# Threshold search with bf16 totals: counts read as their upper 16 bits, each over 256 columns

## The chip, the cores and the metric

The kernel runs on one core of one Trainium2 chip. The metric is the time of one execution on the device, in microseconds (us). A core has five engines with queues of their own: TensorE (PE, with its weight loads listed as PEld), VectorE (DVE), ScalarE (ACT), GpSimd (POOL) and SyncE (SP), which issues transfers. They meet only through semaphores.

## The reference, cut to what matters

A chain of six blocks with residuals on 4 x 1024 tokens of 256 features: an int4 feed-forward, a multi-scale attention, the feed-forward again, a mixture of experts (MoE), a linear attention, and the MoE again with the same weights. The change is in the MoE, which runs twice:

```python
T = 4096; E = 32; cap = int(1.25 * T / E)                # 160
probs = softmax(gelu(ri @ r1_w.T + r1_b) @ r2_w.T)
topp, topi = top_k(probs, 2)
routed = hit.any(1)                                       # the token picked this expert
score = where(routed, probs, -inf)
idx = argsort(-score, axis=0)[:cap].T                     # each expert takes its best 160 tokens
...
xe = xf[idx]; up = xe @ w_up.T; gate, upv = split(up)
ye = (silu(gate) * upv) @ w_down.T
out = zeros.at[idx].add(w * ye)
```

So for each of 32 experts the 160 best of 4096 scores must be found.

## The kernel before, in words

The kernel doesn't sort. Per expert it looks for the score's threshold: the value over which at most 160 scores lie. It does so for 16 experts at a time (a "half", class `Choice`): 128 partitions are 8 parts x 16 experts, and each partition holds 512 scores (`COLS`) of its expert, turned into numbers whose high 16 bits are searched first and then the low ones. One round tries three thresholds at once and gains a factor of four; there are `ROUNDS` = 15 rounds, 7 on the high and 8 on the low bits.

A round k:
- `counts` (VectorE) counts, per partition, how many scores are below the middle threshold, tries[2], over 512 columns (L1442, sum to `under[:, 0:1]`), and with `split` also those below tries[1] over the first 256 columns (L1440, sum to `part`). Then it prepares `ahead` (L1446), the part of the next thresholds that doesn't depend on the outcome.
- `signs` (ScalarE) sums signs of (tries[1] - score), over the second 256 columns with `split` and over 512 without (L1577), and of (tries[3] - score) over 512 columns (L1579), into `under[:, 1:2]` and `under[:, 2:3]`. Counting over a sum of signs is the same up to a factor and a constant.
- `total` (TensorE) adds the 8 parts of each expert and hands every partition the total: a product with `same_e`, a 128x128 matrix of ones and zeros in fp32 as weights, and the sums as 3 moving columns (L1603). With `split` two products come before it into the same PSUM columns: the constant `may_under` (L1598), which moves the limit to zero, and `part` with `twice_e`, which is 2 x same_e (L1600). An fp32 product runs as two passes, each with its own weight load: two records each.
- `decide` (VectorE) compares with the limit (L1452 with `split`; L1454 and L1455 without) and writes the next thresholds (L1456), for which ScalarE, VectorE and TensorE wait.

The first half's search (`split`) runs in `route`, before any expert: nothing else is on TensorE. On VectorE each round has a companion after its counts (`beside(k)`): rounds 3 and 4 make the second half's scores (L2122, L2126), rounds 5 to 8 their sums (L1409), rounds 9 to 13 the tokens' shares. GpSimd works on `values` (L1558, L1560), started once the picks are known. After the search the order is ties, scan, ranks, positions, tables, lists, all on VectorE and TensorE in turns, and then GpSimd gathers the rows of the first experts (L1346).

The second half's search (without `split`) runs in `experts`, laid by `with_steps` into the fixed order of the first 16 experts' work: TensorE runs `up` products (L2369) and `down` products (L2382) of the experts, and a total stands between two `up` pairs. VectorE's product of gate and value (L2493) waits for ScalarE's gate (L2422). All queues are strictly in this order.

The constants (`same_e`, `before_e`, `twice_e`) are made once by GpSimd in `RouterSetup.constants`, at the beginning of the attention.

Of the kernel before, what the change touches and what calls it, by code (L numbers as in the profile page):

```python
# [17 lines left out]
ALU = mybir.AluOpType  # L18
ACT = mybir.ActivationFunctionType
F32 = mybir.dt.float32  # L20
# [5 lines left out]
P = 128  # L26
# [1194 lines left out]
class RouterSetup:  # L1221
# [18 lines left out]
    def constants(self, nc, pool):  # L1240
        s, ints, pool_chain = self.s, self.ints, self.pool_chain
        chain = Chain(pool, pool_chain)
        at = 0
        for out, pattern, base, step in ((s.e_down, [[-1, EXPERTS]], EXPERTS, 0),
                                         (s.tile_no, [[1, 2 * TILES]], 0, 0), (s.row_no, [[0, 1]], 1, 1)):
            n = pattern[0][1]
            chain.link(nc.gpsimd.iota(ints[:, at:at + n], pattern, base=base, channel_multiplier=step))
            chain.link(nc.gpsimd.tensor_copy(out[:], ints[:, at:at + n]))
            at += n
        chain.link(nc.gpsimd.iota(ints[:, at:at + ST_TILES], [[P, ST_TILES]], base=TOKENS + 1, channel_multiplier=1))  # L1250
        chain.link(nc.gpsimd.tensor_copy(s.spare_no[:], ints[:, at:at + ST_TILES]))
        chain.link(nc.gpsimd.tensor_copy(self.mine[:, 0:HALF], s.ident[:, 0:HALF]))
        for j in range(1, PARTS):
            chain.link(nc.gpsimd.tensor_tensor(self.mine[:, 0:HALF], self.mine[:, 0:HALF], s.ident[:, HALF * j:HALF * (j + 1)], ALU.add))
        chain.link(nc.gpsimd.tensor_copy(s.same_e[:].rearrange("p (j e) -> p j e", e=HALF), self.mine[:, 0:HALF].rearrange(
            "p (o e) -> p o e", o=1).broadcast_to([P, PARTS, HALF])))
        chain.link(nc.gpsimd.tensor_copy(s.fold[:], s.ident[:, 0:VALUES * HALF]))
        for j in range(1, P // (VALUES * HALF)):
            chain.link(nc.gpsimd.tensor_tensor(s.fold[:], s.fold[:], s.ident[:, VALUES * HALF * j:VALUES * HALF * (j + 1)], ALU.add))
        chain.link(nc.gpsimd.iota(ints[:, 0:P], [[1, P]], base=1, channel_multiplier=0))  # L1260
        chain.link(nc.gpsimd.tensor_copy(self.mine[:], ints[:, 0:P]))
        chain.link(nc.gpsimd.tensor_scalar(s.before_e[:], self.mine[:], s.row_no[:, 0:1], None, ALU.is_gt))
        chain.link(nc.gpsimd.tensor_tensor(s.before_e[:], s.before_e[:], s.same_e[:], ALU.mult))
        chain.link(nc.gpsimd.tensor_scalar(s.twice_e[:], s.same_e[:], 2.0, None, ALU.mult))
        chain.link(nc.gpsimd.memset(s.half[:], 0.5))
        chain.link(nc.gpsimd.memset(s.tiny[:], 1e-6))
        chain.link(nc.gpsimd.iota(ints[:, at:at + 4], [[1, 4]], base=0, channel_multiplier=0))
        chain.link(nc.gpsimd.tensor_copy(s.tries_no[:], ints[:, at:at + 4]))
        chain.link(nc.gpsimd.memset(s.may_under[:, 0:1], float(CAP - TOKENS) / PARTS))
        chain.link(nc.gpsimd.memset(s.may_under[:, 1:2], float(2 * CAP - TOKENS - TOKENS // 2) / PARTS))  # L1270
        chain.link(nc.gpsimd.memset(s.may_under[:, 2:3], float(2 * CAP - TOKENS) / PARTS))
        chain.link(nc.gpsimd.memset(s.limit[:, 0:1], float(TOKENS - CAP)))
        chain.link(nc.gpsimd.memset(s.limit[:, 1:3], float(TOKENS - 2 * CAP)))
# [9 lines left out]
def alloc_moe(nc, s):  # L1283
    sb = nc.alloc_sbuf_tensor
    s.r1 = sb("r1", [P, CC, HIDDEN], F32)
    s.r1s = sb("r1s", [STATS, HIDDEN], F32)
    s.r1b = sb("r1b", [HIDDEN, 1], F32)
    s.r2 = sb("r2", [HIDDEN, EXPERTS], F32)
    s.e_down = sb("e_down", [P, EXPERTS], F32)
    s.tile_no = sb("tile_no", [P, 2 * TILES], F32)  # L1290
    s.row_no = sb("row_no", [P, 1], F32)
    s.spare_no = sb("spare_no", [P, ST_TILES], F32)
    s.same_e = sb("same_e", [P, P], F32)
    s.before_e = sb("before_e", [P, P], F32)
    s.twice_e = sb("twice_e", [P, P], F32)
    s.half = sb("half", [P, TILES], F32)
    s.tiny = sb("tiny", [P, 1], F32)
    s.tries_no = sb("tries_no", [P, 4], F32)
    s.may_under = sb("may_under", [P, 3], F32)
    s.limit = sb("limit", [P, 3], F32)  # L1300
    s.fold = sb("fold", [P, VALUES * HALF], F32)
    s.xn_rows = nc.dram_tensor("xn_rows", (TOKENS, ROW), F32, kind="Internal").ap()
    s.x_sum = nc.dram_tensor("x_sum", (TOKENS + SPARE, C), F32, kind="Internal").ap()
# [58 lines left out]
class Choice:  # L1362

    def __init__(self, nc, s, m, half, earlier=None):
        self.nc, self.s, self.m, self.half = nc, s, m, half
        st, name = m.st, f"c{half}_"

        def sb(n, shape, dt=F32):  # L1370
            return st.sb(name + n, shape, dt)
        self.score, self.above = sb("score", [P, COLS]), sb("above", [P, COLS])
        if earlier is None:
            self.equal, self.n_above, self.n_equal = (sb(n, [P, COLS]) for n in ("equal", "n_above", "n_equal"))
            self.junk = sb("junk", [P, 2, COLS], BF16)
        else:
            self.equal, self.n_above, self.n_equal, self.junk = earlier.equal, earlier.n_above, earlier.n_equal, earlier.junk
        self.tries, self.ahead = sb("tries", [P, 4]), sb("ahead", [P, 4])
        self.under, self.part, self.passed = sb("under", [P, 3]), sb("part", [P, 1]), sb("passed", [P, 3])
        self.steps, self.level, self.quota, self.one = (sb(n, [P, 1]) for n in ("steps", "level", "quota", "one"))  # L1380
        self.count, self.base = sb("count", [P, 2]), sb("base", [P, 2])
        self.pos = sb("pos", [P, 2, TILES], BF16)
        self.by_place = sb("by_place", [P, CAP])
        self.quads = QUADS_E // 2
        self.tiles = SLOT_TILES // 2
        self.held = sb("held", [P, VALUES, self.tiles])
        self.token = sb("token", [P, self.tiles])
        self.added, self.spare = (sb(n, [P, self.quads, 2, ST_TILES]) for n in ("added", "spare"))
        self.of_any, self.whole = sb("of_any", [P, self.quads, ST_TILES]), sb("whole", [P, self.quads, ST_TILES], I32)
        (self.scored, self.score_turned, self.score_copied, self.halved, self.high_made, self.low_made, self.tried, self.parted,  # L1390
         self.counted, self.signed, self.totaled, self.tied, self.offset, self.placed, self.place_turned, self.pos_made,
         self.valued, self.hot_made, self.slotted, self.copied, self.listed, self.rows_known, self.slots_made, self.dve) = (
            st.sem(name + n) for n in (
                "scored", "score_turned", "score_copied", "halved", "high_made", "low_made", "tried", "parted", "counted", "signed",
                "totaled", "tied", "offset", "placed", "place_turned", "pos_made", "valued", "hot_made", "slotted", "copied", "listed",
                "rows_known", "slots_made", "dve"))
        self.bank, self.score_bank = 4, 6 + half
# [36 lines left out]
    def counts(self, v, k, split):  # L1434
# [4 lines left out]
        if split:  # L1439
            nc.vector.tensor_scalar(self.n_above[:, 0:COLS // 2], self.score[:, 0:COLS // 2], self.tries[:, 1:2], None, ALU.is_lt,  # L1440
                                    ALU.add, accum_out=self.part[:]).then_inc(self.parted, 1)
        nc.vector.tensor_scalar(self.above[:], self.score[:], self.tries[:, 2:3], None, ALU.is_lt, ALU.add,  # L1442
                                accum_out=self.under[:, 0:1]).then_inc(self.counted, 1)
        units = HIGH + LOW
        unit = 0.5 if k + 1 in (len(HIGH), ROUNDS) else float(units[k + 1])
        nc.vector.tensor_scalar(self.ahead[:], self.s.tries_no[:], unit, self.tries[:, 0:1], ALU.mult, ALU.add)  # L1446
# [147 lines left out]
    def total(self, pe, k, split):  # L1594
        nc, s, totals = self.nc, self.s, self.s.ps[:, self.bank, 0:3]
        pe.wait_ge(self.tried, self.turn_of(k))
        if split:
            nc.tensor.matmul(totals, s.same_e[:], s.may_under[:], start=True, stop=False, skip_group_check=True)  # L1598
            pe.wait_ge(self.parted, k + 1)
            nc.tensor.matmul(totals[:, 1:2], s.twice_e[:], self.part[:], start=False, stop=False, skip_group_check=True)  # L1600
        pe.wait_ge(self.counted, k + 1)
        pe.wait_ge(self.signed, k + 1)
        nc.tensor.matmul(totals, s.same_e[:], self.under[:], start=not split, stop=True,  # L1603
                         skip_group_check=True).then_inc(self.totaled, 1)

    def offsets(self, pe):
        nc, s = self.nc, self.s
# [1417 lines left out]
```

## Time and profile before

| | before |
|---|---|
| median of 3 runs | 1800.84 us (1800.36 to 1804.57) |
| profiled execution | 1800.5 us, of which span 1798.8 us |
| TensorE busy | 1506.6 us (84%) |
| VectorE busy | 968.8 us (54%) |
| ScalarE busy | 729.0 us (41%) |
| GpSimd busy | 563.1 us (31%) |
| mean granted TensorE clock | 0.907 |

The profile is of one execution; its records name engine, line, operation and tiles. "Idle before" is the idle time of the engine in front of a record, with what ended it. A group whose records repeat is merged, with its count. The ends of TensorE's records are modelled. Granted clock 1.00 is 2.4 GHz, 0.50 is 1.2 GHz.

### The profile page before, as it was taken

The numbers are of one execution on the slowest core, as the hardware profiler recorded it, in microseconds if no ns is written. First come the engines' busy times: TensorE is split into PE (matmuls) and PEld (weight loads), VectorE is DVE, ScalarE is ACT, GpSimd is POOL, SyncE is SP. The second block draws the span as 40 slices with busy tenths as digits, with TensorE's granted clock in tenths as the row PEclk, the third lists the DMA queues.
The fourth block names the chain that finished last, engine by engine and source line by source line (L and its number), as shares of the span: only waits on it lengthen the run. The fifth ranks groups of instructions, "written<-read, shape, count | busy, mean of one in ns | idle before, by whom it ended". The sixth has DMA issues, their size and how long they took to land. (4 is left out here: it accounts for less than half of the span.)

```text
span 1798.8 us, 26975 instructions
## 1 busy us (share of the span) xinstructions
PE 1506.6 (84%) x9512; PEld 1150.9 (64%) x9512; DVE 968.8 (54%) x2696; ACT 729.0 (41%) x1775; POOL 563.1 (31%) x466
## 2 busy tenths in 40 slices
PE   6899989999998677549999996589995559999994
PEld 5566544555554554439989996355553549899994
DVE  8766677787883597755531111356565754521110
ACT  4222147666666385415323232123433425322331
POOL 6522200000000441221646445222111231637545
PEclk9998989999999898559999998799996569999997
DMA  3042462333300031325879974410113225879974
GB/s 103 18 144 111 119 125 55 78 55 79 55 26 2 19 111 62 146 46 187 229 205 248 257 230 64 129 36 24 47 47 124 76 71 191 231 215 248 265 193 46
DMA packets 113492, 212.10 MB, mean 118 GB/s; under 512 B 20085, under 2 KB 79386, under 8 KB 104154
## 3 DMA queue, kind: packets, MB, share of 16 engines
q1 hardware_dynamic: 87066, 178.93, 31.4%
q0 software_dynamic: 26304, 31.60, 11.5%
q8 instruction: 69, 1.13, 0.3%
q14 instruction: 53, 0.43, 0.1%
HBM read 158.71 MB, written 51.38 MB: 117 GB/s over the span
## 5 line engine op out<-in xcount | busy, mean ns | idle before, releaser
L952 DVE TENSOR_REDUCE attnm_top<-psum 128x1 f32<-128x384 f32 (+3 forms) x384 | 212.9, 597 | 56.7 <-PE psum L1037 52.6
L1174 ACT ACTIVATE attnm_prob<-psum 128x512 f32<-128x512 f32 (+1 forms) x384 | 192.1, 530 | 88.8 <-PE psum L1047 82.2
L2493 DVE SCALAR_TENSOR_TENSOR moe2e_h<-moe2e_gate,psum 128x160 f32<-128x160 f32 x160 | 50.6, 321 | 203.0 <-ACT moe2e_gate L2422 173.4
L2314 POOL DMA_INDIRECT out<-moe2e_y,moe_scatter_i x76 | 118.7, 1562 | 130.9 <-ACT moe2e_y L2448 69.9
L2493 DVE SCALAR_TENSOR_TENSOR moe1e_h<-moe1e_gate,psum 128x160 f32<-128x160 f32 x160 | 50.6, 321 | 202.6 <-ACT moe1e_gate L2422 161.0
L2314 POOL DMA_INDIRECT x_sum<-moe1e_y,moe_scatter_i x76 | 119.1, 1567 | 129.3 <-ACT moe1e_y L2448 71.5
L2369 PE MATMUL psum<-moe2e_xgT,moe_w_up 128*128 128x160 f32 x1024 | 152.4, 304 | 2.4 <-ACT moe2e_xgT L2438 2.4
L2369 PE MATMUL psum<-moe1e_xgT,moe_w_up 128*128 128x160 f32 x1024 | 152.2, 304 | 2.4 <-ACT moe1e_xgT L2438 2.4
L2369 PEld LDWEIGHTS psum<-moe2e_xgT,moe_w_up 128*128 128x128 f32 x1024 | 144.0, 193 | 4.8 <-issue 4.8
L2369 PEld LDWEIGHTS psum<-moe1e_xgT,moe_w_up 128*128 128x128 f32 x1024 | 143.9, 193 | 4.8 <-issue 4.8
L1346 POOL DMA_INDIRECT moe_xg<-xn_rows,moe_gather_i x80 | 84.3, 1054 | 168.3 <-DVE moe_gather_i L1531 102.0
L938 POOL TENSOR_TENSOR attnm_tail_v<-attnm_v_tail,attnm_tail_p 128x256 f32<-128x256 f32 x32 | 19.8, 620 | 343.9 <-PE psum L1089 284.4
L1035 PE MATMUL psum<-attn_mask_ts,ident_bf 128*128 128x128 bf16 x512 | 105.4, 226 | 10.2 <-DVE attnm_top L952 7.8
L1037 PE MATMUL psum<-attnm_k_hat,attnm_q_hat 96*128 96x512 bf16 (+3 forms) x384 | 107.2, 307 | 0.0
L1047 PE MATMUL psum<-attnm_q_hat,attnm_k_hat 99*128 99x512 bf16 (+1 forms) x288 | 98.5, 345 | 1.3 <-ACT attnm_prob L1174 0.6
L2422 ACT ACTIVATE moe1e_gate<-psum 128x160 f32<-128x160 f32 x160 | 47.3, 301 | 104.4 <-PE psum L2369 91.0
L2422 ACT ACTIVATE moe2e_gate<-psum 128x160 f32<-128x160 f32 x160 | 47.4, 301 | 103.8 <-PE psum L2369 91.0
L1035 PEld LDWEIGHTS psum<-attn_mask_ts,ident_bf 128*128 128x128 bf16 x512 | 50.1, 100 | 50.0 <-issue 24.3
L2382 PE MATMUL psum<-moe1e_h,moe_w_down 128*128 128x160 f32 x512 | 80.4, 300 | 2.1 <-ACT moe1e_yT L2430 1.2
L2382 PE MATMUL psum<-moe2e_h,moe_w_down 128*128 128x160 f32 x512 | 80.4, 300 | 2.1 <-ACT moe2e_yT L2430 1.2
L1060 PE MATMUL psum<-attnm_prob,attn_v_aug 128*32 128x512 f32 (+1 forms) x768 | 78.7, 527 | 0.0
L2382 PEld LDWEIGHTS psum<-moe2e_h,moe_w_down 128*128 128x128 f32 x512 | 72.9, 190 | 2.8 <-ACT moe2e_yT L2430 1.6
(407 smaller groups left out, 3246.9 us busy)
## 6 DMA issues: line engine op xcount, KB each, us to landing
moe_w_up<-in_expert_up SPq DMA_DIRECT2D x64, 1024.0 KB
moe_w_down<-in_expert_down SPq DMA_DIRECT2D x64, 512.0 KB
attnm_q_hat<-q_parts SPq DMA_DIRECT2D x72, 128.0 KB, 4.6
moe_a_up<-in_adapter_up SPq DMA_DIRECT2D x32, 256.0 KB
q_parts<-attnf_q_part SPq DMA_DIRECT2D x12, 512.0 KB, 2.8
attnm_k_hat<-k_parts SPq DMA_DIRECT2D x72, 64.0 KB, 2.3
x_res<-in_x SPq DMA_DIRECT2D x8, 512.0 KB, 8.3
v_tails<-attnf_v_tail SPq DMA_DIRECT2D x4, 1024.0 KB, 4.3
```

The costliest lines, as they stand in the source:

```text
L952: nc.vector.tensor_reduce(top[:, n // QUADS % 2, tiles[0]:tiles[-1] + 1, hh:hh + 1], s.ps[:, u.bank, 0:len(tiles) * width].rearrange("p (t ...
L1035: nc.tensor.matmul(out[:, width - P:width], s.identb[:], o.mask_ts[:, tile % 2, :], start=(i == 0), stop=False, skip_group_check=True)
L1037: ins = nc.tensor.matmul(out, q_hat[r][0:MROW, h, tile * P:(tile + 1) * P], k_hat[r][0:MROW, h, 0:width], start=False, stop=True, skip_gro ...
L1047: nc.tensor.matmul(s.ps[:, u.bank, at:GROUP], k_hat[r][0:MROW + NPART, h, j * P:(j + 1) * P], q_hat[r][0:MROW + NPART, h, g * GROUP + at:( ...
L1060: ins = nc.tensor.matmul(s.ps[32 * h:32 * h + 32, u.bank, at:GROUP], o.v_aug[:, first:first + 32], prob[:, i % NPROB, at:GROUP], start=(j ...
L1174: nc.scalar.activation(prob[:, i % NPROB, at:GROUP], s.ps[:, u.bank, at:GROUP], ACT.Exp).then_inc(taken[u.bank], 1)
L1346: pool.indirect_dma_start(self.xg[:, q, k, :], None, self.rows, bass.IndirectOffsetOnAxis(ap=self.gather_i[:, at:at + 1], axis=0), bounds_ ...
L2314: nc.gpsimd.indirect_dma_start(total, bass.IndirectOffsetOnAxis(ap=rows, axis=0), y[:, q, k, :], None, bounds_check=TOKENS + SPARE - 1, oo ...
L2369: ins = nc.tensor.matmul(s.ps[:, u.bank, half * CAP:(half + 1) * CAP], lhsT, xgT[:, q, c, k * CAP:(k + 1) * CAP], start=(c == 0), stop=(c ...
L2382: ins = nc.tensor.matmul(s.ps[:, u.bank, o * CAP:(o + 1) * CAP], lhsT, h[:, n % 2, i, :], start=(i == 0), stop=(i == PAIRS - 1))
L2422: nc.scalar.activation(gate[:, i, :], s.ps[:, u.bank, 0:CAP], ACT.Silu).then_inc(silu, 1)
L2493: nc.vector.scalar_tensor_tensor(out=h[:, n % 2, i, :], in0=gate[:, i, :], scalar=1.0 if i < INTER // P else SCALE_A, in1=s.ps[:, u.bank, ...
```

## The change

Every count is now over 256 columns, so it is a whole number of at most 256, and the sign sums are whole numbers from -256 to 256, or even ones up to 512: all of them are exact in bf16, and in the fp32 word their lower 16 bits are zero. The products that total them read only the upper 16 bits of each fp32 word, as bf16 with a step of two, and take bf16 weights (`same_b`, `twice_b`). For that, the 512-column count becomes two counts of 256 columns, whose sums lie in `under[:, 0:1]` and in a new column `under[:, 3:4]`, each with its own semaphore step. With `split` TensorE multiplies the first half's count, the second half's count, and then the two sign sums: three bf16 products in place of one fp32 product, and `part` as bf16 too; `may_under` stays fp32. Without `split` there are two bf16 products, both after all the sums. GpSimd makes one more constant.

```diff
-        chain.link(nc.gpsimd.tensor_scalar(s.twice_e[:], s.same_e[:], 2.0, None, ALU.mult))
+        chain.link(nc.gpsimd.tensor_copy(s.same_b[:], s.same_e[:]))
+        chain.link(nc.gpsimd.tensor_scalar(s.twice_b[:], s.same_e[:], 2.0, None, ALU.mult))
...
-    s.twice_e = sb("twice_e", [P, P], F32)
+    s.same_b = sb("same_b", [P, P], BF16)
+    s.twice_b = sb("twice_b", [P, P], BF16)
...
-        self.under, self.part, self.passed = sb("under", [P, 3]), sb("part", [P, 1]), sb("passed", [P, 3])
+        self.under, self.part, self.passed = sb("under", [P, 4]), sb("part", [P, 1]), sb("passed", [P, 3])
+        self.under_b, self.part_b = (of[:].bitcast(BF16)[:, 1::2] for of in (self.under, self.part))
...
-        nc.vector.tensor_scalar(self.above[:], self.score[:], self.tries[:, 2:3], None, ALU.is_lt, ALU.add,
-                                accum_out=self.under[:, 0:1]).then_inc(self.counted, 1)
+        for i, half in enumerate((slice(0, COLS // 2), slice(COLS // 2, COLS))):
+            nc.vector.tensor_scalar(self.above[:, half], self.score[:, half], self.tries[:, 2:3], None, ALU.is_lt, ALU.add,
+                                    accum_out=self.under[:, 3 * i:3 * i + 1]).then_inc(self.counted, 1)
...
-            nc.tensor.matmul(totals[:, 1:2], s.twice_e[:], self.part[:], start=False, stop=False, skip_group_check=True)
-        pe.wait_ge(self.counted, k + 1)
-        pe.wait_ge(self.signed, k + 1)
-        nc.tensor.matmul(totals, s.same_e[:], self.under[:], start=not split, stop=True,
-                         skip_group_check=True).then_inc(self.totaled, 1)
+            nc.tensor.matmul(totals[:, 1:2], s.twice_b[:], self.part_b, start=False, stop=False, skip_group_check=True)
+            for i in range(2):
+                pe.wait_ge(self.counted, 2 * k + i + 1)
+                nc.tensor.matmul(totals[:, 0:1], s.same_b[:], self.under_b[:, 3 * i:3 * i + 1], start=False, stop=(i == 1),
+                                 skip_group_check=True)
+            pe.wait_ge(self.signed, k + 1)
+            nc.tensor.matmul(totals[:, 1:3], s.same_b[:], self.under_b[:, 1:3], start=False, stop=True,
+                             skip_group_check=True).then_inc(self.totaled, 1)
+        else:
+            pe.wait_ge(self.counted, 2 * k + 2)
+            pe.wait_ge(self.signed, k + 1)
+            nc.tensor.matmul(totals, s.same_b[:], self.under_b[:, 0:3], start=True, stop=False, skip_group_check=True)
+            nc.tensor.matmul(totals[:, 0:1], s.same_b[:], self.under_b[:, 3:4], start=False, stop=True,
+                             skip_group_check=True).then_inc(self.totaled, 1)
```

## Rows read from the trace of the kernel before

**Rows 1.** The page: TensorE's granted clock, in tenths, in 40 slices.
```profile
PEclk9998989999999898559999998799996569999997
```
**Rows 2.** Table by stretches: length, busy time (records) by engine, clock, DMA, GB/s.
```profile
728.00:748.00 20.00, 11.77 (x43) 10.52 (x42) 16.35 (x61) 10.36 (x30) 12.30 (x9) 0.50 0.31 126
1500.00:1545.00 45.00, 44.37 (x334) 44.09 (x332) 23.86 (x88) 23.18 (x75) 17.45 (x12) 1.00 0.75 224
```
**Rows 3.** Timeline, early search, round 5: start us, length us, engine, line.
```profile
743.63 0.48 DVE L1440 TENSOR_SCALAR_CACHE_REDUCE moe_c_n_above<-moe_c_score,moe_c_tries 128x256 f32<-128x256 f32 x1
744.03 0.74 DVE L1442 TENSOR_SCALAR_CACHE_REDUCE moe_c_above<-moe_c_score,moe_c_tries 128x512 f32<-128x512 f32 x1
744.70 0.08 DVE L1442 DVE_READ_ACCUMULATOR moe_c_above<-moe_c_score,moe_c_tries 128x1 f32 x1
744.75 0.18 ACT L1579 ACTIVATION_READ_ACCUMULATOR moe_c_junk<-moe_c_score,moe_c_tries 128x1 f32 x1
744.83 0.28 DVE L1409 SCALAR_TENSOR_TENSOR moe_c_above<-moe_w_down,moe_prob 128x128 f32<-128x128 f32 x1
745.04 0.50 PEld L1603 LDWEIGHTS psum<-moe_c_under,same_e 128*128 128x128 f32 x2 [0.37 <-DVE moe_c_above L1442]
745.08 0.56 PE L1603 MATMUL psum<-moe_c_under,same_e 128*128 128x3 f32 x2 [0.32 <-ACT moe_c_junk L1579]
746.07 0.48 DVE L1440 TENSOR_SCALAR_CACHE_REDUCE moe_c_n_above<-moe_c_score,moe_c_tries 128x256 f32<-128x256 f32 x1
```
**Rows 4.** Timeline, fp32 products at 1.2 GHz, with 128 and with 32 weight columns.
```profile
789.40 0.64 PE L1635 MATMUL psum<-fold,moe_c_by_place 128*128 128x32 f32 x2 [0.39 <-ACT moe_c_by_place L1584]
789.96 0.32 PE L1636 MATMUL psum<-fold,moe_c_by_place 128*32 128x32 f32 x2
```
**Rows 5.** Timeline at 2.4 GHz in the attention: fp32, then bf16 products, in a row.
```profile
510.57 0.38 PE L1089 MATMUL psum<-ident,attnm_tail_v 128*128 128x128 f32 x2
510.69 0.10 PEld L1035 LDWEIGHTS psum<-attn_mask_ts,ident_bf 128*128 128x128 bf16 x1
510.80 0.22 PE L1035 MATMUL psum<-attn_mask_ts,ident_bf 128*128 128x128 bf16 x1
510.85 0.33 PE L1037 MATMUL psum<-attnm_k_hat,attnm_q_hat 96*128 96x384 bf16 x1
```
**Rows 6.** Timeline, early search, round 2, beside GpSimd's work on values.
```profile
736.25 1.05 POOL L1558 TENSOR_TENSOR moe_value<-moe_pick,tile_no 128x512 bf16<-128x512 f32 x1
736.52 0.81 DVE L1446 TENSOR_SCALAR moe_c_ahead<-tries_no,moe_c_tries 128x4 f32<-128x4 f32 x1
737.50 0.16 DVE L1452 TENSOR_SCALAR_CACHE_REDUCE moe_c_passed<-psum 128x3 f32<-128x3 f32 x1 [0.17 <-PE psum L1603]
```
**Rows 7.** Timeline, early search, rounds 4 and 11 (its counts began at 760.01).
```profile
742.29 0.69 DVE L2126 TENSOR_TENSOR moe_prob<-moe_prob,moe_a_down 128x512 f32<-128x512 f32 x1
743.23 0.16 DVE L1452 TENSOR_SCALAR_CACHE_REDUCE moe_c_passed<-psum 128x3 f32<-128x3 f32 x1 [0.25 <-PE psum L1603]
...
761.22 0.35 DVE L2158 RECIPROCAL moe_a_down<-moe_a_down 128x32 f32<-128x32 f32 x1
```
**Rows 8.** Timeline, late search, VectorE: the experts' product after a round's counts.
```profile
1478.81 0.55 DVE L2493 SCALAR_TENSOR_TENSOR moe2e_h<-moe2e_gate,psum 128x160 f32<-128x160 f32 x2 [0.84 <-ACT moe2e_gate L2422]
```
**Rows 9.** The chain that ended last: expert passes with two totals, and without.
```profile
1505.29 1.09 PE psum L2369 x8
1506.38 0.12 PE psum L1603 x2
...
1511.17 2.72 PE psum L2382 x20
...
1605.71 5.43 PE psum L2369 x40
```
**Rows 10.** Timeline, GpSimd: its next work after the constants, which end at 229.5.
```profile
288.99 1.20 POOL L938 TENSOR_TENSOR attnm_tail_v<-attnm_v_tail,attnm_tail_p 128x256 f32<-128x256 f32 x2 [59.51 <-DVE attnm_tail_p L980]
```
**Rows 11.** Groups from 728 to 768 us: loads of L1603: count, busy us, mean ns, idle.
```profile
L1603 PEld LDWEIGHTS psum<-moe_c_under,same_e 128*128 128x128 f32 x28 | 7.0, 311 | 5.2 <-DVE moe_c_above L1442 5.2
```

## The prediction

> **What bounds the kernel now.** I read the page first: TensorE is busy 84% of the span, and its clock line [rows 1] has dips, the ones at slices 17 and 32 of 40 among them. The table by stretches [rows 2] says what they are: the two searches of the first expert half (about 729 to 770 us and 1395 to 1435 us). There TensorE is granted 0.50 of its clock, 1.2 GHz, and is busy 11.8 of 20 us; no engine is full. Such a stretch is bound by a loop of dependencies, round by round. In the searches of the second half (about 1469 to 1538 us, and the same in the first MoE block) the granted clock is 1.00, 2.4 GHz, and TensorE is busy 44.4 of 45 us: there TensorE's own stream is the bound. So one edit has two prices. In all, 15 rounds, two halves, two MoE blocks: 30 rounds of each kind.
>
> One round alone [rows 3], from the new thresholds at 743.63 (t = 0): VectorE counts 256 columns (L1440), starts the 512-column count (L1442) at 0.40, and its sum is read by 1.15. ScalarE's second sign sum is read by 1.30 (744.75 + 0.18 - 743.63). TensorE loads same_e at 1.41, in two fp32 passes, and the product ends at 2.01 (745.08 + 0.56). VectorE then decides (L1452, L1456), and the next round starts at 2.44. ScalarE's sign sum is the last arrival; after it, 0.60 us of the product's two passes lie bare on the path.
>
> **The early searches, part by part.** Removed: one of the two passes of that last product. What a pass costs at 1.2 GHz: two passes with 128-column fp32 weights take 0.64 us, two with 32-column weights 0.32 [rows 4]. The difference of 0.32 over 2 x 96 columns is 1.7 ns a column, so a 128-column fp32 load costs 0.21 of the path, and the fixed rest of L1603 is 0.60 - 2 x 0.21 = 0.17. No row has a 128-column bf16 load at this clock. From below it is free (a tail of 0.17), from above it costs the fp32 load (0.21 + 0.17 = 0.38). I take one element per cycle, half of fp32, 0.11 (tail 0.28), since bf16 products of 128 columns follow each other every 0.05 us at 2.4 GHz [rows 5], so their loads fit into 0.05 there.
>
> Added on VectorE: the 512-column count becomes two of 256. The first 256-column count takes 0.40 until the next starts, so the third starts at 0.81 and its sum is there by 0.81 + 0.40 + 0.08 = 1.29, against 1.15 before: 0.14 later, and just ahead of ScalarE's 1.30. From the end of ScalarE's read to the load 0.11 us pass [rows 3]; VectorE's signal I put at 0.06, since here the load waits for one semaphore only, not for two, so the product of the second half count can begin to load at 1.35. Added on TensorE: this product stands right in front of the last one. It loads until 1.46, the last one until 1.57, and ends at 1.74, against 2.01: a gain of 0.27. The product of the first half count is ready at about 0.95 and is hidden under the wait for ScalarE. Ends for the gain: with both loads at the fp32 price 1.35 + 0.21 + 0.21 + 0.17 = 1.94, a gain of 0.07; with free loads, and ScalarE's sum then the limit at 1.41, a tail of 0.17, a gain of 0.43. I take 0.30, between 0.27 and the upper end, because half of fp32's price is only what the spacing of 0.05 allows at most.
>
> Where it does not come through: VectorE must be free by then. In rounds 5 to 8 (counted from 0) L1409 ends at 1.48 [rows 3], 1.62 after, ahead of the 1.74 at which L1452 would start: full gain. Of the companions of rounds 9 to 14 the one that ends last, L2158's reciprocal, ends at 1.56 [rows 7], 1.70 after, ahead of 1.74 too. In rounds 0 to 3 GpSimd works on `values`, and L1446 takes 0.81 us instead of 0.23, ending with GpSimd's L1558 (737.33 against 736.25 + 1.05); L1452 starts 0.17 after that [rows 6]. GpSimd's series is started before the search and does not get shorter, so the 0.15 won in round 0 is not won again, and in round 3 the 0.69 of L2122 follows L1446 with no idle time: I count zero for these four. In round 4 L2126 ends at 742.98 and L1452 starts 0.25 later [rows 7]; 0.14 of that is eaten by the longer count, which leaves about 0.06. So 10 rounds x 0.30 + 0.06 = 3.1 us a search, 6.1 us for both. After the search everything is a chain on VectorE and moves with it; the first gather waits for it.
>
> **The late searches.** VectorE's count is also 0.14 longer, but the products of the experts that follow it (L2493) wait 0.84 for ScalarE's gate [rows 8], which hides it; if that cover were gone it would cost up to 0.14 a round. On TensorE: 40 fp32 expert passes with two totals in between run from 1505.29 to 1511.17, 5.88 us; without totals 40 take 5.43 [rows 9]. So one total costs 0.22 us, two bare 128-column fp32 loads at 2.4 GHz. After the change there are two bf16 products. In the stream an expert pass of 160 columns (0.136 us) hides the load behind it; the load of the second product and the fp32 load of the next expert pass lie bare: 0.05 + 0.11 = 0.16, a gain of 0.06. Ends: no gain (fp32-priced loads), or both products at nothing and the next load hidden, 0.22; I stay near the first, at 0.055 for 30 rounds, 1.6 us. A change from fp32 to bf16 costs nothing visible: L1035 starts 0.23 after L1089's two fp32 passes did, which is two loads of 0.11 [rows 5].
>
> The extra instruction on GpSimd (a copy of 128x128 into bf16) falls into the preparation, which ends at 229.5 us; GpSimd's next work starts at 289, after 59.5 us of idle time [rows 10]. It costs nothing.
>
> **The sum.** The profiled execution took 1800.5 us (1798.8 of span and 1.7 around it); the median of the three runs is 1800.84, so the two may stand for each other. 1800.5 - 6.1 - 1.6 = 1792.8.
>
> **The rivals.**
> (A) Loads do not overlap. If the last load could only begin when the second half count's product is through, the round ends at 1.35 + 0.11 + 0.17 + 0.11 + 0.17 = 1.91: a gain of 0.10, 20 x 0.10 = 2.0 us, and nothing late: 1798.5, no change that can be measured. For it: all four products have the same weights' place and the same PSUM columns. Against it: the two loads of L1603 take 0.50 us in all [rows 3] where one is 0.31 long [rows 11], so the second began 0.19 in, before the first product could have ended. The Trainium skill ("TensorE: Matmul & The Clock Gate", Part 3: Packing small matmuls) has this rule, that a load overlaps running products only in other row groups; L1603's rows speak against it.
> (B) bf16 loads cost half of what I take. A bf16 load record is 0.10 us long at 2.4 GHz for 128 columns [rows 5], half of what one of fp32 takes so a price of 0.05 and all below it is open. With half (0.055 at 1.2 GHz) the two loads end at 1.46 and the product at 1.63: a gain of 0.38; ten rounds twice and round 4, 7.7 us; late 0.08 a total, 2.4 us: 1800.5 - 10.1 = 1790.4. The Trainium skill (same page, Weight-path perf modes) says that bf16 weights of 128 columns are loaded about twice as fast as otherwise, and fp32 ones are not; no row here isolates it.
> (C) Slower. VectorE becomes the last arrival: if a count had to be read out before the next one starts, each of 256 columns would take 0.48 + 0.08 = 0.56. The third sum would come at 1.68, the last product end at 1.74 + 0.11 + 0.11 + 0.17 = 2.13, 0.12 later than now, 3.6 us in 30 rounds; late the two counts would take 1.12 instead of 0.83, and where the gate comes early and the cover of 0.84 is gone, 30 x 0.29 = 8.7 us: 1812.8. Early, it turns slower from a third sum at 1.56 on. Against it: L1442 starts 0.40 after L1440 with exactly such a read between them.
> (D) The change does its work but a hidden floor (the gate, GpSimd's series, or the wait for ScalarE) takes half of the early gain: 3 + 1 = 4 us, 1796.5. Also no measurable change.
>
> **How the numbers follow.** 0.3% is 5.4 us, about what a measurement of this kernel can tell from no change: the border is 1795.4. My forecast 0.50, B 0.20, A 0.12, D 0.15, C 0.03. All of B and nearly all of the forecast are faster; some hundredths of it fall short: faster 0.67, same 0.30, slower 0.03. B to D are 1790.4 to 1796.5; a little past both, for the ends of the two load prices, the range is 1788.5 to 1798.0.
>
> **What would show it.** In the profile after: at 1.2 GHz single bf16 passes in place of pairs; the period of rounds 5 to 8 at 2.14 instead of 2.44; rounds 1 and 2 still at 2.57, with L1446 at 0.8; L1603's second half product starting at 1.35 and the last one not before it; late, two totals over 40 expert passes at 5.77 instead of 5.88. I am wrong if the third count's sum comes well after 1.30, if the last product's load waits for the one before it, or if rounds 0 to 3 get shorter too.

## The result, and the profile after

| | before | after |
|---|---|---|
| median of 6 runs each, timed in turns | 1802.38 us | 1786.9 us (1784.81 to 1790.26) |
| ratio, with its 95% interval | | 0.9919 [0.9906, 0.9931] |
| profiled execution | 1800.5 us | 1788.87 us, of which span 1787.2 us |
| mean granted TensorE clock | 0.907 | 0.908 |

The changed kernel is faster, by 15.5 us between these medians and by 11.6 us between the two profiled executions; 7.7 us were predicted. The same kernel was timed twice more beside the experiments and gave 13.1 and 11.4 us there, both times a ratio of 0.9931.

The kernel after has other line numbers: L1444 is the count for `part`, L1447 the two half counts, L1451 `ahead`, L1457 and L1461 the decision, L1603 `may_under`, L1605 `part`, L1608 the half counts' products, L1611 the product of the sign sums; L1616 and L1617 are the two products of a late total, L2383 and L2396 the experts' `up` and `down`; L1582 and L1584 are ScalarE's sign sums, L1563 and L1565 GpSimd's values, L1468 and L1469 the ties, and L1480 and L1485 VectorE's scans and the product behind them, after the ties. In the kernels of the experiments these numbers move by a few lines.

The first page line to read beside [rows 1] is the clock of the kernel after, 40 slices in tenths. The dips stand at the same slices.

```profile
PEclk9989889999999898559999999699997569999997
```

The table by stretches of the kernel after, with the columns of [rows 2]. In the early search the clock is 1.2 GHz as before, and TensorE is busy 8.53 of 20 us, before 11.77.

```profile
728.00:748.00 20.00, 8.53 (x43) 6.37 (x43) 16.97 (x74) 9.75 (x29) 12.30 (x9) 0.50 0.40 162
```

The timeline of round 5 of an early search in the kernel after, the round of [rows 3] (start us, length us, engine, line). It begins at 745.30.

```profile
745.30 0.48 DVE L1444 TENSOR_SCALAR_CACHE_REDUCE moe_c_n_above<-moe_c_score,moe_c_tries 128x256 f32<-128x256 f32 x1
...
746.10 0.47 DVE L1447 TENSOR_SCALAR_CACHE_REDUCE moe_c_above<-moe_c_score,moe_c_tries 128x256 f32<-128x256 f32 x1
746.24 0.10 PEld L1608 LDWEIGHTS psum<-moe_c_under,same_b 128*128 128x128 bf16 x1 [0.29 <-DVE moe_c_above L1447]
...
746.42 0.19 ACT L1584 ACTIVATION_READ_ACCUMULATOR moe_c_junk<-moe_c_score,moe_c_tries 128x1 f32 x1
746.50 0.08 DVE L1447 DVE_READ_ACCUMULATOR moe_c_above<-moe_c_score,moe_c_tries 128x1 f32 x1
...
746.64 0.11 PEld L1608 LDWEIGHTS psum<-moe_c_under,same_b 128*128 128x128 bf16 x1 [0.29 <-DVE moe_c_above L1447]
746.64 0.19 PE L1608 MATMUL psum<-moe_c_under,same_b 128*128 128x1 bf16 x1 [0.21 <-DVE moe_c_above L1447]
746.65 0.12 PEld L1611 LDWEIGHTS psum<-moe_c_under,same_b 128*128 128x128 bf16 x1
746.69 0.17 PE L1611 MATMUL psum<-moe_c_under,same_b 128*128 128x2 bf16 x1
746.90 0.16 DVE L1457 TENSOR_SCALAR_CACHE_REDUCE moe_c_passed<-psum 128x3 f32<-128x3 f32 x1
...
747.30 0.48 DVE L1444 TENSOR_SCALAR_CACHE_REDUCE moe_c_n_above<-moe_c_score,moe_c_tries 128x256 f32<-128x256 f32 x1
```

Counted from the round's start: VectorE's third sum is there at 1.28, ScalarE's at 1.31, the second half count's load starts at 1.34 and the last load at 1.35, and the last product ends at 1.56. Before, the two passes began at 1.41 and ended at 2.01 [rows 3]. The period is 2.00 instead of 2.44.

Read in this way, each round of an early search has these periods (us, from one start of the first count to the next; rounds 0 to 13, the first MoE block; the second block has the same to within 0.05):

| round | 0 | 1 | 2 | 3 | 4 | 5 | 6 | 7 | 8 | 9 | 10 | 11 | 12 | 13 |
|---|---|---|---|---|---|---|---|---|---|---|---|---|---|---|
| before | 2.54 | 2.57 | 2.56 | 3.08 | 2.54 | 2.44 | 3.97 | 2.45 | 2.45 | 2.54 | 2.53 | 2.54 | 2.54 | 2.45 |
| after | 2.53 | 2.57 | 2.56 | 3.08 | 2.46 | 2.00 | 3.52 | 2.00 | 2.00 | 2.10 | 2.10 | 2.12 | 2.08 | 2.00 |

Round 6 is the longest, before and after, since the low bits are prepared between its decision and the next count. From the first count to the ties the search takes 35.31 and 35.35 us (first and second block), before 39.83 and 39.87: 9.04 us in both together.

The chain of work that ended last, late search, of the kernel after (start us, length us, what), which answers to [rows 9].

```profile
1494.66 1.09 PE psum L2383 x8
1495.74 0.00 PE psum L1616
1495.75 0.02 PE psum L1617
1495.77 3.37 PE psum L2383 x24
1499.14 0.00 PE psum L1616
1499.15 0.02 PE psum L1617
1499.17 1.20 PE psum L2383 x8
1500.37 1.77 PE psum L2396 x13
...
1594.46 5.43 PE psum L2383 x40
```

40 expert passes with two totals take 1500.37 - 1494.66 = 5.71 us, without totals 5.43: a total costs 0.14, before 0.22. 30 totals x 0.08 = 2.4 us. This counts every total as if it lay on the chain. The stretches themselves agree: from the early ties to the late ties, both blocks together, six profiles with the late part of the change (the changed kernel three times, the late part alone, and the kernels with four more products and with a second wait) have 204.0 to 205.6 us, and the two with the late search of before have 207.0 and 207.9. The two stages give 9.04 + 2.4 = 11.4 us, which is the difference of the profiled executions, 11.6, but for 0.2. Other stretches, which the change does not touch, differ by more than that and cancel: the first search starts at 732.10, before at 730.34, 1.8 us later, and the linear attention up to the second search takes 286.2 us (1104.8 to 1390.97), before 287.6 (1108.0 to 1395.61), 1.4 less.

### The profile page after: what moved, and what is told of

Its sections match the earlier page's. It is cut to its first block and busy times, and to the rows that moved or that the text cites. A ratio compares the mean times of both kernels' runs of the same rounds, so it can differ in the third digit from the quotient of the medians.

```text
span 1787.2 us, 27066 instructions
## 1 busy us (share of the span) xinstructions
PE 1488.8 (83%) x9512; PEld 1127.3 (63%) x9512; DVE 977.1 (55%) x2816; ACT 728.9 (41%) x1775; POOL 564.3 (32%) x467
## 3 DMA queue, kind: packets, MB, share of 16 engines
q0 software_dynamic: 26304, 31.60, 11.4%
## 5 line engine op out<-in xcount | busy, mean ns | idle before, releaser
L2383 PE MATMUL psum<-moe1e_xgT,moe_w_up 128*128 128x160 f32 x1024 | 152.2, 304 | 2.4 <-ACT moe1e_xgT L2452 2.4
L2383 PE MATMUL psum<-moe2e_xgT,moe_w_up 128*128 128x160 f32 x1024 | 150.7, 302 | 2.4 <-ACT moe2e_xgT L2452 2.4
L2383 PEld LDWEIGHTS psum<-moe1e_xgT,moe_w_up 128*128 128x128 f32 x1024 | 144.2, 193 | 4.8 <-issue 4.8
L2383 PEld LDWEIGHTS psum<-moe2e_xgT,moe_w_up 128*128 128x128 f32 x1024 | 142.7, 192 | 4.8 <-issue 4.8
L1037 PE MATMUL psum<-attnm_k_hat,attnm_q_hat 96*128 96x512 bf16 (+3 forms) x384 | 107.4, 308 | 0.0
L2396 PE MATMUL psum<-moe2e_h,moe_w_down 128*128 128x160 f32 x512 | 80.4, 300 | 2.1 <-ACT moe2e_yT L2444 1.2
L2396 PE MATMUL psum<-moe1e_h,moe_w_down 128*128 128x160 f32 x512 | 80.4, 300 | 2.1 <-ACT moe1e_yT L2444 1.2
L2396 PEld LDWEIGHTS psum<-moe2e_h,moe_w_down 128*128 128x128 f32 x512 | 72.9, 190 | 2.8 <-ACT moe2e_yT L2444 1.6
```

The lines of the kernel that those rows point to most:

```text
L1037: ins = nc.tensor.matmul(out, q_hat[r][0:MROW, h, tile * P:(tile + 1) * P], k_hat[r][0:MROW, h, 0:width], start=False, stop=True, skip_gro ...
L2383: ins = nc.tensor.matmul(s.ps[:, u.bank, half * CAP:(half + 1) * CAP], lhsT, xgT[:, q, c, k * CAP:(k + 1) * CAP], start=(c == 0), stop=(c ...
L2396: ins = nc.tensor.matmul(s.ps[:, u.bank, o * CAP:(o + 1) * CAP], lhsT, h[:, n % 2, i, :], start=(i == 0), stop=(i == PAIRS - 1))
```

## The experiments

Two theories stood against each other after the result. L: the gain is the cheap load; a 128-column bf16 load costs a few hundredths of a us where the fp32 one costs 0.21 at 1.2 GHz. O: it is the order; the counts are multiplied beforehand, and the last product waits for one semaphore instead of two and has two moving columns instead of three. Below, a gain in us is against the median of the kernel before in the same group of runs: 1802.71 for the first four, 1802.9 for the next four, 1801.98 for the last three.

**The change's order with fp32 products.** All else is as after.

```diff
-nc.tensor.matmul(totals[:, 1:2], s.twice_b[:], self.part_b, ...)
+nc.tensor.matmul(totals[:, 1:2], s.twice_e[:], self.part[:], ...)
-nc.tensor.matmul(totals[:, 1:3], s.same_b[:], self.under_b[:, 1:3], ...)
+nc.tensor.matmul(totals[:, 1:3], s.same_e[:], self.under[:, 1:3], ...)
```
(and the same for the half counts and the two late products)

> The changed kernel with every total back in fp32: halved counts, the order of the products and the waits stay as in the change. Theory L (a bf16 load of 128 columns is nearly free, an fp32 one costs 0.21 us a pass at 1.2 GHz): the last two products then have four bare loads behind a second half count at 1.34, so the early round of 2.44 before and 2.00 after becomes 2.7 to 2.8, and a late total, 0.22 before and 0.14 after, becomes about 0.43; in all some 14 us over the kernel before, 1816. Rival O (the gain is from the order: counts out of the last product, one wait on each): the early round stays below 2.44, and the kernel is at or below the time before, 1795 to 1803.

Measured: 1817.11 us, ratio 1.0092 [1.0071, 1.0114], slower than before. The rounds that took 2.00 take 2.85, rounds 0 to 3 take 2.85 too, and a search 44.87. Its timeline, round 8, which started at 750.09 (L1609 is its last product):

```profile
751.29 0.08 DVE L1445 DVE_READ_ACCUMULATOR moe_c_above<-moe_c_score,moe_c_tries 128x1 f32 x1
751.86 0.55 PEld L1609 LDWEIGHTS psum<-moe_c_under,same_e 128*128 128x128 f32 x2
751.93 0.56 PE L1609 MATMUL psum<-moe_c_under,same_e 128*128 128x2 f32 x2
```

The last sum is read at 1.28, but the last load starts at 1.77, behind four fp32 loads of the half counts, of which two could start only with that sum, and its product ends at 2.40. The same late chain as above, of this kernel:

```profile
1494.83 1.09 PE psum L2381 x8
1495.92 0.12 PE psum L1614 x2
1496.04 0.22 PE psum L1615 x2
```

A late total has 0.34 in place of 0.12 before and 0.02 to 0.03 after. So the order, with its halved counts and added product, costs 5.04 us a search and 0.22 a late total as long as the products are fp32: O alone gives no gain, and without the bf16 type there is none. That the order is worth nothing with bf16 products does not follow from this run. The form that would tell, all sums in one bf16 product behind both waits in the early search, was not run; one part of the order, the wait, is tested below. The time also shows that not every late total is worth its price: from ties to ties both blocks take 3.9 us longer, not 30 x 0.22 = 6.6, and with the 10.05 of the searches that is 14.0 of the 14.4 us.

**Each half of the change alone.** In the first kernel the late search has the 512-column count and one fp32 product as before; in the second the early search has.

```diff
+if split:   # early: two half counts, bf16 products
+else:       # late: one 512-column count, one fp32 product, as before
```

> The change in the early searches alone; the late ones as before, with one count of 512 columns and one fp32 product. By the stretches of the two profiles the early searches gave 4.5 us each, 9.0 us in all, and the late ones about 0.08 a total, 2.4 us. If these sums are the whole effect: 1802.4 - 9.0 = 1793.4, ratio 0.995. If the change also shortens something outside the searches (the medians lie 15.5 us apart, the two profiles 11.6), and that comes with the early part, it is 1789 to 1790.

> The change in the late searches alone; the early ones as before. If the stretches are the whole effect: 30 totals x 0.08 = 2.4 us, 1800.0, ratio 0.9987, with early rounds of 2.44 and 40 expert passes with two totals in 5.71 instead of 5.88. If the late part carries the gain that the stretches do not show, 1796 or less.

> The changed kernel itself once more, beside its two halves on the same chip. If the stretches are the whole effect, the ratio is 0.9936 (11.5 us), at the near end of the interval measured first (0.9906 to 0.9931), and equals the product of the two halves' ratios. If there is more to it, 0.9915 again.

Measured: early alone 1790.28 us, ratio 0.9937 [0.9921, 0.9952]; late alone 1800.04, 0.999 [0.9981, 0.9999]; the whole change in the same group 1789.63, 0.9931 [0.9915, 0.9946]. The product of the two halves is 0.9937 x 0.999 = 0.9927, so they add up. The early edit gives 0.0063 x 1802.7 = 11.4 us with an interval of 8.7 to 14.2, in which the 9.04 of the searches' lengths lies; the late one 1.8 us (0.2 to 3.4), and 2.4 lies in that. The lengths and the late chains change only where the edit is: a search is 35.32 and 35.36 long with early alone, 39.82 and 40.10 with late alone (there, in the second block, round 4 took 2.78 instead of 2.54, which nothing in the edit explains). The chain of the first has the total of before, that of the second the total of after:

```profile
1499.62 0.12 PE psum L1620 x2
```

```profile
1500.29 0.01 PE psum L1617
1500.29 0.02 PE psum L1618
```

So no third effect beside the two stages is needed; the 15.5 us of the first timing is more than both, and was not found again.

**Four more bf16 products** in front of the last one, into the same PSUM bank but other columns, which nothing reads. They carry `start=True`, and with them the kernel no longer gives the right result; why was not settled. The number of rounds is fixed, so what is read here is their length.

```diff
+for i in range(4):
+    nc.tensor.matmul(s.ps[:, self.bank, 8 + 2 * i:10 + 2 * i], s.same_b[:], self.under_b[:, 1:3], start=True, stop=True, ...)
 nc.tensor.matmul(totals[:, 1:3], s.same_b[:], self.under_b[:, 1:3], start=False, stop=True, ...)
```

> The changed kernel with four more bf16 products of two columns (weights same_b) in front of each early round's last product, behind the wait for the sign sums; they write PSUM columns that nothing reads. It measures what one bf16 load and product costs on the path at 1.2 GHz. As I predicted it (0.11 us a load): plain rounds of 2.00 become 2.43. Theory L as the profile after suggests (the last load starts 0.01 after the one before): 2.05 to 2.20, that is 0.01 to 0.05 for each.

Measured (one run): 1791.8 us. The rounds of 2.00 take 2.10, so one bf16 product with its load of 128 columns costs 0.10 / 4 = 0.025 us at 1.2 GHz. Its timeline, round 6, which started at 743.57 (L1608 is the second half count's product, L1612 the four added ones, L1614 the last one):

```profile
744.92 0.19 PE L1608 MATMUL psum<-moe_c_under,same_b 128*128 128x1 bf16 x1 [0.21 <-DVE moe_c_above L1447]
744.93 0.20 PEld L1612 LDWEIGHTS psum<-moe_c_under,same_b 128*128 128x128 bf16 x4
744.97 0.25 PE L1612 MATMUL psum<-moe_c_under,same_b 128*128 128x2 bf16 x4
745.05 0.10 PEld L1614 LDWEIGHTS psum<-moe_c_under,same_b 128*128 128x128 bf16 x1
```

Five loads start between 744.93 and 745.05, one every 0.03 us, while a single record is 0.10 long. This is the disputed price by itself: 0.025, where the prediction took 0.11, four times as much. An fp32 pass's load costs 0.21 at this clock [rows 4], eight times as much. The Trainium skill ("TensorE: Matmul & The Clock Gate", Weight-path perf modes) gives about a factor of two for the fast loading of 128 weight columns in bf16 and no gain for fp32; the factor of eight here is that between the two types.

**A second wait** on the last product, for the half counts that are already there.

```diff
+pe.wait_ge(self.counted, 2 * k + 2)
 pe.wait_ge(self.signed, k + 1)
 nc.tensor.matmul(totals[:, 1:3], s.same_b[:], self.under_b[:, 1:3], ...)
```

> The changed kernel in which the last product of an early round waits for two semaphores again (that of the counts, which is already satisfied, and that of the signs), as before the change. In the profile before, 0.11 us passed from the end of ScalarE's read to the load, after it 0.04. If the second wait costs that difference, plain rounds of 2.00 become 2.06 to 2.09; if the difference is chance or comes from the format, they stay at 2.00.

Measured (one run): 1791.53 us, rounds of 2.05 and 2.06 instead of 2.00. The timeline of round 6, which started at 744.51 (L1612 is its last product):

```profile
745.63 0.19 ACT L1584 ACTIVATION_READ_ACCUMULATOR moe_c_junk<-moe_c_score,moe_c_tries 128x1 f32 x1
...
745.85 0.10 PEld L1608 LDWEIGHTS psum<-moe_c_under,same_b 128*128 128x128 bf16 x1 [0.30 <-DVE moe_c_above L1447]
...
745.93 0.10 PEld L1612 LDWEIGHTS psum<-moe_c_under,same_b 128*128 128x128 bf16 x1
```

From the end of ScalarE's read, 745.82, to the load it is 0.11, as in [rows 3] with its two waits; after the change it is 0.04. With two waits the profile has one of them as an instruction of its own in TensorE's queue, ahead of the load (the view of line L1611, with ns min/median/max):

```profile
L1611 PEldq EVENT_SEMAPHORE  x30: 51/51/51, 730.6 to 1425.2; - x30
```

The kernel before has the same instruction of 51 ns at each of its 60 totals (L1602), the kernel after at its 30 late ones only (L1615). So a second wait costs 0.055 us on the path, although the product in front has waited for the same counts already. That much of O holds.

**One count of 512 columns**, read as bf16, with one product for it instead of two (late one product for all sums). Counts over 256 lose their last bit, so this kernel leaves out the exactness of the thresholds.

```diff
-for i, half in enumerate((slice(0, COLS // 2), slice(COLS // 2, COLS))):
-    nc.vector.tensor_scalar(self.above[:, half], self.score[:, half], self.tries[:, 2:3], ...)
+nc.vector.tensor_scalar(self.above[:], self.score[:], self.tries[:, 2:3], ...)
```

> The changed kernel with VectorE's count over 512 columns in one piece again, its sum read as bf16 all the same. Counts over 256 then lose their last bit, so thresholds can be off: this part of the computation is not exact here. It separates the price of the halved counts. If the 0.14 us are hidden behind ScalarE (third sum at 1.28, sign sum at 1.31), plain rounds stay at 2.00 (1.99 to 2.01), round 4, which VectorE bounds, falls from 2.46 to about 2.35, rounds 0 to 3 stay. If VectorE is the last arrival after the change, plain rounds fall to 1.95 or less. The late total falls from 0.14 by 0.02, one product fewer.

Measured (one run): 1790.95 us, the rounds of 2.00 take 1.98 to 1.99, and round 4 takes 2.32 instead of 2.46. Halving the count costs next to nothing in ten rounds, since ScalarE's sum comes last in any case, and 0.14 in round 4, where VectorE's own queue is the path. A late total has one product of 0.01 us in the chain, or less, in place of two of 0.02 to 0.03 together, as expected.

**GpSimd's values moved.** The first four rounds gained nothing. First both halves' products were moved behind the ties:

```diff
+pool.wait_ge(first.tied, 1)
 pool.wait_ge(m.picked, 1)
 first.values(pool)
-second.values(pool)
...
 late.lows(pool)
+late.values(pool)
```

> The changed kernel with GpSimd's work on `values` moved out of the search: the first half's starts at the ties, the second half's in the experts. It tests the floor that I put under rounds 0 to 3. If GpSimd sets it: rounds 0 to 2 fall from 2.57 to 2.00, round 3 from 3.08 to about 2.4, 2.4 us a search and 4.8 in all: 1789.6 - 4.8 = 1784.8, ratio 0.9905 to before. Rival: the floor is only moved, because values beside the scans is not ready when the positions need it, or because GpSimd's gathers come later: then the search is as much shorter and the time is 1788 to 1790.

Measured: 1788.3 us, ratio 0.9913 [0.9898, 0.9929]. Rounds 0 to 3 take 1.99, 2.00, 2.00 and 2.34, and both searches 32.88: 2.43 and 2.47 us less each. So GpSimd was their floor. The time, though, is that of the rival in the expectation: what was moved lies beside the scans now. Its timeline behind the search:

```profile
766.27 1.05 POOL L1563 TENSOR_TENSOR moe_value<-moe_pick,tile_no 128x512 bf16<-128x512 f32 x1 [33.59 <-DVE moe_c_equal L1469]
767.55 1.52 DVE L1480 TENSOR_TENSOR_SCAN moe_c_n_above<-moe_c_one,moe_c_base,moe_c_above 128x512 f32<-128x512 f32 x1
769.11 1.89 DVE L1480 TENSOR_TENSOR_SCAN moe_c_n_equal<-moe_c_one,moe_c_base,moe_c_equal 128x512 f32<-128x512 f32 x1
771.04 1.00 DVE L1485 SCALAR_TENSOR_TENSOR moe_c_equal<-moe_c_n_equal,moe_c_quota,moe_c_equal 128x512 f32<-128x512 f32 x1
```

and the same in the kernel after, where GpSimd is idle:

```profile
770.20 1.28 DVE L1480 TENSOR_TENSOR_SCAN moe_c_n_above<-moe_c_one,moe_c_base,moe_c_above 128x512 f32<-128x512 f32 x1
771.52 1.28 DVE L1480 TENSOR_TENSOR_SCAN moe_c_n_equal<-moe_c_one,moe_c_base,moe_c_equal 128x512 f32<-128x512 f32 x1
772.84 0.75 DVE L1485 SCALAR_TENSOR_TENSOR moe_c_equal<-moe_c_n_equal,moe_c_quota,moe_c_equal 128x512 f32<-128x512 f32 x1
```

0.24 + 0.61 + 0.25 = 1.10 us: the way from the ties to the first gather is 1.1 longer (23.88 instead of 22.80), and each search keeps 1.3 of its 2.4.

**Only the second half's values moved**, to stand beside the first experts, with the change itself and the version above in the same group.

```diff
 first.values(pool)
-second.values(pool)
...
 late.lows(pool)
+late.values(pool)
```

> The change itself once more, beside the two kernels of this group that move GpSimd's products of the picks. The stage sum of the two traces (9.04 us in the early searches, 2.5 us in the totals of the late one) gives 11.5 us below the kernel before; the two timings so far gave 15.5 and 13.1 us. Expected 1790, and both early searches 35.3 long.

> Only the second half's two pairs of products of the picks (L1563, L1565) leave the early searches, for the place behind the ties beside the first half's experts; the first half's two stay at the search's start. They cover rounds 0 and 1 with their 5.2 us, so theory (GpSimd is the floor of the first four rounds) expects 2.54 in rounds 0 and 1, and 2.0 and 2.3 in rounds 2 and 3: a length of 34.0 in place of 35.3 in each early search, and the scans behind the ties at 1.28 again (1.5 and 1.9 in the kernel that moved both). So 2.6 us below the change: 1787.4. If what was moved delays the first half's experts, their stage gives some of it back.

> Both halves' products moved behind the ties, timed beside the change this time. The length of the early searches is 32.9 and the way from the ties to the gather 1.1 us longer than in the change: by the stages 2 x (2.43 - 1.1) = 2.7 us below the change, 1787.3, no better and no worse than moving the second half's alone.

Measured: the change 1790.6 us (1789.52 to 1793.29), ratio 0.9931 [0.9918, 0.9945]; the second half's values moved 1784.13 (1781.23 to 1785.95), 0.9897 [0.988, 0.9913]; both moved 1786.04, 0.9901 [0.9886, 0.9917]. The timeline of the second kernel, early search, whose rounds 0 to 3 start at 730.77, 733.32, 735.89 and 737.88:

```profile
734.12 1.05 POOL L1563 TENSOR_TENSOR moe_value<-moe_pick,tile_no 128x512 bf16<-128x512 f32 x1
734.52 0.67 DVE L1451 TENSOR_SCALAR moe_c_ahead<-tries_no,moe_c_tries 128x4 f32<-128x4 f32 x1
735.15 1.56 POOL L1565 TENSOR_SCALAR moe_value<-moe_pick,row_no 128x512 bf16<-128x512 f32 x1
...
737.09 0.22 DVE L1451 TENSOR_SCALAR moe_c_ahead<-tries_no,moe_c_tries 128x4 f32<-128x4 f32 x1
```

L1451 takes 0.67 while GpSimd multiplies and 0.22 once it has ended; the rounds take 2.55, 2.57, 1.99 and 2.34, the searches 34.01 and 34.06, as expected. Both moves beat the change, whose interval lies above theirs, for the version with both moved by 0.0001 only. They do so by 6.5 and 4.6 us, though, where the stages show 2.6 and 2.7. Between the profiles of the change and of the second kernel in this group the rest lies in stretches that the edit does not shorten: 1.2 us ahead of the first search, 4.1 between the first gather and the second search. In the second of these stretches the three profiles of the change itself differ by 2.6 us (600.2 to 602.9, here 598.8), and the moved values lie in it. Whether the rest belongs to the edit or is chance was not settled. The version with the second half's values moved is the fastest that was run; between it and the one with both moved the intervals overlap.

## Why the prediction fell short

**What bounds the kernel.** Right in both places: a loop of dependencies at 1.2 GHz in the early searches, TensorE's stream at 2.4 GHz in the late ones. Early alone and late alone gave the two prices separately.

**The price of a bf16 load, the step that failed.** "I take one element per cycle, half of fp32, 0.11" stood on the spacing of 0.05 at 2.4 GHz [rows 5]. But the prediction itself said that this spacing is what the price is at most. Those products have 128 moving columns, and the columns fill the spacing: L1037 of [rows 5], with 384, starts at 510.85, 0.17 before the next product in the timeline of before, three times as much.

```profile
511.02 0.38 PE L1047 MATMUL psum<-attnm_q_hat,attnm_k_hat 99*128 99x512 bf16 x1
```

Measured: 0.025 us at 1.2 GHz (four more products), and 0.01 from the second half count's load to the last one. The last product ends at 1.56, not at 1.74, and the round gains 0.44, not 0.30. In terms of the sum, with the wait of the next paragraph: 10 rounds x 2 searches x 0.14 = 2.8 us.

**The signal and the wait.** Half of it was right. VectorE's sum was expected at 1.29 and the second half count's load at 1.35; they came at 1.28 and 1.34. That a single wait is quicker was used for this load and left out for the last one, since the loads in front seemed to cover it; with cheap loads it counts, 0.055 us of the 0.44 (the second wait).

**The parts of 0.44.** From ScalarE's read to the load 0.11 became 0.04, and load to end of product 0.60 became 0.21; 0.01 later is the end of ScalarE's read. 0.07 + 0.39 - 0.01 = 0.45, the 0.44 of the periods but for rounding. The upper end of the prediction's own span, 0.43 with free loads, comes closest, partly by luck: it had the last load at 1.41 and a tail of 0.17, which gives 1.58; measured are 1.35 and 0.21, which gives 1.56. The tail fits within 0.02: 0.17 + 0.025 is 0.20.

**Where it does not come through.** Rounds 0 to 3 stayed as they were and round 4 gained 0.08 (0.06 predicted), and the cause was the one named: with GpSimd's values gone from rounds 2 and 3 they fall to 1.99 and 2.34.

**The late searches.** Mechanism right, size small by the same price: 0.05 + 0.11 for the second product and the next expert load was taken, 0.03 + 0.11 was measured. 30 x 0.025 = 0.8 us. The cover of the longer count by the gate held: in the second block's late search the counts are in neither chain. The chain leaves TensorE for the gate and the decision of a round at the start of the search (1475.90 to 1478.73 before, 1461.89 to 1468.70 after, where it is two rounds) and once more in the middle (1514.99 to 1518.55 before, 1504.18 to 1507.74 after, both 3.6 us); both times it runs over the gate, the decision and ScalarE's sign sums.

**The rivals.** A (loads wait for products) is refuted: the last load starts 0.01 after the load before it, when that one's product has 0.18 still to run. The Trainium skill's rule for it ("TensorE: Matmul & The Clock Gate", Part 3: Packing small matmuls) fails here, since all these products have the same rows. B was the right direction and still too dear. It leaned on the length of a load's record, 0.10 and half of an fp32 one; [rows 5] shows no fp32 load, those of L1089 are 0.14 long on average, and a bf16 record is 0.10 long at 1.2 GHz too, where loads start every 0.03: the length of the record is not the price. In numbers B gave 0.38 a round and 1790.4 us; the rounds gained 0.44, and 1800.5 - 11.4 = 1789.1. C did not happen: a count starts 0.40 after the one before it, each time. D happened only in the rounds that had been set to zero already.

**The range.** The first median, 1786.9, lies 1.6 us below it. Its low end, 1788.5, had room for the price of a free load in the early rounds and little else: the sum of the stages, 1789.1, and the two later medians lie within it. It left out the spread of a median itself, which for this kernel is 1786.9, 1789.63 and 1790.6 in three timings. So of the 5.9 us between forecast and first median some 3.7 are the load's price and the wait, and some 2.2 are in no stage of the trace.

## What to carry to other kernels

Where two prices are open between "half" and "nothing", look at what fills the row that the middle value comes from: a spacing that the moving columns fill says nothing of the load. On a path of small products, cut the last product's passes and its waits first, and put everything that is ready earlier in front of it, if it is bf16; the same order in fp32 made this kernel slower. And before a series on GpSimd is left beside VectorE's short instructions, ask whether its results are wanted there: here the place of least harm was beside the first experts.

## What the hardware showed that was not expected

- A bf16 load of 128 columns with a product of two columns behind another such costs 0.025 us at 1.2 GHz, while its load's record is 0.10 long; the load of one fp32 pass costs 0.21. At 2.4 GHz, between expert passes, two bf16 products take 0.02 to 0.03, and one in fp32 0.12 behind an expert pass and 0.22 behind another product.
- A second semaphore wait in front of a product is an instruction of 0.051 us in TensorE's queue, and costs 0.055 us on the path of the early rounds.
- GpSimd beside VectorE: a 128x4 instruction takes 0.67 instead of 0.22, scans of 128x512 take 1.52 and 1.89 instead of 1.28, and a 128x512 product of two steps 1.00 instead of 0.75.
